# A graph network in which the second middle attention layer goes from gathered edges to a dense sum over all sources

## The chip, the cores and the metric

One core of one Trainium2 chip. The time is device microseconds of one execution of the program; the median of three runs is given. Five engines work side by side and wait for each other through semaphores: PE (TensorE, matmuls), DVE (VectorE), ACT (ScalarE), POOL (GpSimd) and SP (SyncE, here only a DMA queue). The chip has 128 partitions in SBUF and PSUM, and PSUM has 8 banks of 512 fp32 columns.

## The reference

The graph has 3125 nodes with 256 features and 103,125 directed edges (50,000 random pairs in both directions, and a loop at every node). Four graph layers follow each other, each with a residual and a layer norm: a transformer convolution, a relation layer, a two-step graph attention ("L2") and a last layer with attention and a scan. The change is about the second attention of L2 (one head), cut here to what is computed:

```python
feat = h1 @ fc2_w.T                                   # [n, 256]
el = sum(feat * attn_l2, -1); er = sum(feat * attn_r2, -1)
e  = leaky_relu(el[src] + er[dst], 0.2)
ex = exp(e - segment_max(e, dst)[dst])
a  = ex / segment_sum(ex, dst)[dst]
h2 = segment_sum(feat[src] * a, dst) + bias2
x  = layernorm(x + h2 + norm * (concat([inputs, h1]) @ wb1.T + bb1))
```

An edge that occurs twice counts twice in both sums.

## The kernel before, in words

Nodes are sorted by the number of their edges and laid into T = 25 tiles of P = 128 (NP = 3200 places). Every node of a tile is one partition. `build_slots` writes for each tile a list of records to a scratch tensor `slots`: one record holds 16 source numbers for each of the 128 nodes, as two chunks of S = 8. The most connected node of a tile sets how many chunks the tile has; there are 116 chunks in all, in 64 records.

The program then runs stages, each closed by `finish` (clear the semaphores, a barrier of all engines): count edges, order nodes, project and build the slots, and the layers `conv`, `rel`, `gat1`, `gat2`, `last`, `join`. Three of them are made by one function, `edge_layer` (line 907), with other sizes. Per chunk in `gat2`, `gather` on POOL (line 1012) issues 8 indirect DMAs (line 1021), each of which fetches for all 128 nodes one source row of 257 numbers (256 features and el) from DRAM. SP loads the 8 source numbers and the mask of a chunk (lines 995, 998). DVE makes the logits (`logits`, lines 1086 to 1092), ACT the exponentials (line 1252), and DVE multiplies the 8 rows by their weights (line 1100) and adds them up (a reduce that reads with a step of 256 numbers, lines 1110 and 1112), with a running maximum and rescaling (lines 1113 to 1127). Three buffers of rows let POOL run ahead. At the first two chunks of a tile the tile before is finished: division, bias, the part held in `kp["a"]`, residual, norm (lines 1135 to 1158, 755, 756), PE transposes the new x and multiplies it by the next layer's weights (lines 724, 732), ACT copies the result to `stage`, POOL scatters it to DRAM (lines 1030, 1034). Everything is fp32. The order on each engine is the order of the program; there is no planner.

`count_edges` (line 108) already counts by one-hot products: DVE compares bf16 numbers with a row of iotas (line 183), and PE multiplies the two one-hot matrices (line 221).

## Time and profile before

| | |
|---|---|
| median of 3 runs | 7950.94 us (7949.7 to 7951.02) |
| the profiled execution | span 7951.9 us, which is the only time that its page has |
| DVE busy | 5588.3 us, 70% |
| POOL busy | 5351.3 us, 67% |
| PE busy (matmul) | 3326.4 us, 42% |
| ACT busy | 1251.3 us, 16% |

The page gives busy time over the whole span; the stages have different limits, so it is read by stretch. "PEclk" is TensorE's granted clock in tenths of 2.4 GHz: 5 means 1.2 GHz. In a timeline, a row is a start and a duration; consecutive instructions on one engine overlap a little, so what an instruction costs in a chain is the distance from its start to the next start. On SP and in rows with a q behind the engine the duration is the issue alone.

### The profile page before, as it was taken

How to read it: one execution, taken by the hardware profiler on the slowest of the kernel's cores; microseconds unless marked ns; L12 is line 12 of the kernel's file. 1: busy time of each engine (PE TensorE's matmuls, PEld its weight loads, DVE VectorE, ACT ScalarE, POOL GpSimd, SP SyncE). 2: the span in 40 equal slices, each digit the busy share in tenths (PEclk: the TensorE clock that was granted, in tenths of full speed). 3: DMA queues.
4: the chain of work that ended last, by engine and by line, in shares of the span. 5: the costliest groups of instructions: out<-in, count | busy, mean ns of one | idle time of the engine just before them, and what ended most of it. 6: DMA issues, size and time to landing. Idle time of an engine off the chain costs nothing. (4 is left out here: it accounts for less than half of the span.)

```text
span 7951.9 us, 73782 instructions
## 1 busy us (share of the span) xinstructions
PE 3326.4 (42%) x15180; PEld 2659.3 (33%) x15181; DVE 5588.3 (70%) x11215; ACT 1251.3 (16%) x2729; POOL 5351.3 (67%) x4985
## 2 busy tenths in 40 slices
PE   3445454444677767212222200000025555555556
PEld 3233333334666666101111100000024444444434
DVE  7578888884333343688888677777766778777756
ACT  3101111111011111000000000001022332222312
POOL 0667676665777777577777677777757777776521
PEclk7766767667878888555555555555557787777767
DMA  2346656552332332233333233333322333333210
GB/s 84 88 129 169 165 154 166 161 142 76 85 88 84 86 88 76 64 92 97 88 98 93 65 79 98 90 89 98 86 82 84 112 105 104 107 103 96 76 35 13
DMA packets 489232, 773.99 MB, mean 97 GB/s; under 512 B 298796, under 2 KB 319767, under 8 KB 485436
## 3 DMA queue, kind: packets, MB, share of 16 engines
q0 software_dynamic: 265920, 667.09, 30.5%
q10 hardware_dynamic: 20536, 77.34, 2.6%
q1 hardware_dynamic: 202688, 28.69, 2.3%
q14 instruction: 69, 0.57, 0.0%
q8 instruction: 19, 0.31, 0.0%
HBM read 823.08 MB, written 46.52 MB: 109 GB/s over the span
## 5 line engine op out<-in xcount | busy, mean ns | idle before, releaser
L1021 POOL DMA_INDIRECT gat_rows<-scratch_gat,gat_index x1856 | 1858.4, 1001 | 583.4 <-issue 542.4
L1934 POOL DMA_INDIRECT m_rows<-scratch_gat,m_index x928 | 1217.9, 1312 | 508.8 <-issue 272.9
L1021 POOL DMA_INDIRECT conv_rows<-scratch_kv,conv_index x928 | 929.8, 1002 | 424.4 <-issue 252.1
L1467 POOL DMA_INDIRECT rel_rows<-scratch_x,rel_index x928 | 1016.0, 1095 | 295.4 <-issue 279.4
L1317 PE MATMUL conv_ps<-conv_work,k_ident 128*128 128x256 f32 x1856 | 679.2, 545 | 751.1 <-DVE conv_work L1100 679.5
L724 PE MATMUL gat_ps<-k_ident,gat_cur 128*128 128x128 f32 x100 | 34.5, 448 | 2127.7 <-DVEq L1184 1201.7
L1317 PEld LDWEIGHTS conv_ps<-conv_work,k_ident 128*128 128x128 f32 x1856 | 520.5, 288 | 910.2 <-issue 721.1
L724 PEld LDWEIGHTS gat_ps<-k_ident,gat_cur 128*128 128x128 f32 x100 | 14.5, 203 | 2163.3 <-DVEq L1184 1220.1
L1732 PE MATMUL rel_ps<-rel_factor,rel_rows 128*128 128x128 f32 x3712 | 600.3, 338 | 270.6 <-DMA rel_rows<-scratch_x,rel_index 270.3
L1732 PEld LDWEIGHTS rel_ps<-rel_factor,rel_rows 128*128 128x128 f32 x3712 | 582.5, 251 | 282.7 <-DMA rel_rows<-scratch_x,rel_index 175.1
L1112 DVE TENSOR_REDUCE gat_red<-gat_work 128x256 f32<-128x2048 f32 x182 | 652.4, 3584 | 0.0
L1100 DVE TENSOR_TENSOR gat_work<-gat_rows,gat_psprob 128x2048 f32<-128x2048 f32 x232 | 530.8, 2288 | 61.9 <-ACT gat_psprob L1252 50.4
L1990 PE MATMUL m_ps<-m_work,k_ident 128*128 128x256 f32 x1664 | 491.6, 464 | 172.3 <-DVE m_work L2224 172.3
L1990 PEld LDWEIGHTS m_ps<-m_work,k_ident 128*128 128x128 f32 x1664 | 391.1, 240 | 261.2 <-issue 190.9
L1974 PE MATMUL m_ps<-m_hs,k_ident 128*128 128x128 f32 x1600 | 281.9, 358 | 318.8 <-DVEq L2193 318.8
L1974 PEld LDWEIGHTS m_ps<-m_hs,k_ident 128*128 128x128 f32 x1600 | 272.4, 270 | 333.6 <-DVEq L2193 333.6
L1252 ACT ACTIVATE gat_psprob<-gat_logit 128x72 f32<-128x72 f32 (+1 forms) x232 | 48.2, 208 | 2129.7 <-DVE gat_logit L1092 2129.7
L1083 DVE TENSOR_TENSOR conv_dots<-conv_rows,conv_psown 128x2048 f32<-128x2048 f32 x116 | 265.4, 2288 | 84.2 <-DMA conv_rows<-scratch_kv,conv_index 36.6
L2224 DVE TENSOR_TENSOR m_work<-m_rows,m_ps 128x2048 f32<-128x2048 f32 x104 | 238.0, 2289 | 80.2 <-ACT m_ps L2056 80.2
L1100 DVE TENSOR_TENSOR conv_work<-conv_rows,conv_psprob 128x2048 f32<-128x2048 f32 x116 | 265.2, 2286 | 21.4 <-ACT conv_psprob L1252 20.4
L1084 DVE TENSOR_REDUCE conv_logit<-conv_dots 128x64 f32<-128x2048 f32 x116 | 265.2, 2286 | 4.0
L1528 DVE TENSOR_TENSOR rel_ps<-rel_ps,rel_norm 128x128 f32<-128x128 f32 x65 | 19.3, 296 | 321.4 <-PE rel_ps L1720 321.3
(488 smaller groups left out, 7569.5 us busy)
## 6 DMA issues: line engine op xcount, KB each, us to landing
m_bc<-scratch_bc ACTq DMA_DIRECT2D x25, 2048.0 KB, 8.6
gat_rows<-scratch_gat,gat_index POOLq DMA_INDIRECT x1856
conv_rows<-scratch_kv,conv_index POOLq DMA_INDIRECT x928
rel_rows<-scratch_x,rel_index POOLq DMA_INDIRECT x928
m_rows<-scratch_gat,m_index POOLq DMA_INDIRECT x928
scratch_runs<-e_runs_sb ACTq DMA_DIRECT2D x1, 6453.1 KB
scratch_runs<-e_runs_sb SPq DMA_DIRECT2D x1, 6437.5 KB
scratch_kv<-p_row ACTq DMA_DIRECT2D x25, 256.0 KB, 2.5
```

The source lines that it names most:

```text
L1021: pool.indirect_dma_start(out=rows[b][:, s, :], out_offset=None, in_=table, in_offset=bass.IndirectOffsetOnAxis(ap=index[b][:, s:s + 1], a ...
L1083: st.do(v.tensor_tensor(dots[:], rows[b][:, :, 0:F], over_slots(own[:], S), ALU.mult))
L1084: st.do(v.tensor_reduce(lg, dots[:].rearrange(per_head, h=H), X, ALU.add))
L1100: v.tensor_tensor(work[b][:].rearrange(per_head, h=H), rows[b][:, :, values:values + F].rearrange(per_head, h=H), over_dims(prob[:, 0:S, : ...
L1112: st.add(v.tensor_reduce(red[:], slots, X, ALU.add))
L1317: ins = pe.matmul(ps_sum[min(b, 1)], ident, work[b][:, s, :], start=s == 0, stop=s == S - 1)
L1467: pool.indirect_dma_start(out=rows[b][:, g, :], out_offset=None, in_=dr["x1"], in_offset=bass.IndirectOffsetOnAxis(ap=index[b][:, g:g + 1] ...
L1732: ins = pe.matmul(ps_sums[h * 2 + g // 4][:, (g % 4) * P:(g % 4 + 1) * P], rows[b][:, g, h * P:(h + 1) * P], factor[b][:, g * BASES:(g + 1 ...
L1934: pool.indirect_dma_start(out=rows[b][:, s, :], out_offset=None, in_=dr["gat3"], in_offset=bass.IndirectOffsetOnAxis(ap=index[b][:, s:s + ...
L1974: ins = pe.matmul(ps_y[:, k, :], kp["ident"][:], hs[:, k, n, :], start=n == 0, stop=n == NS - 1)
L1990: ins = pe.matmul(ps_sum[bank_of(b)], kp["ident"][:], work[b][:, s, :], start=s == 0, stop=s == S - 1)
L2224: v.tensor_tensor(work[b].rearrange(per_head, h=H), rows[b][:, :, 0:F].rearrange(per_head, h=H), over_dims(prob[:, 0:S, :], D), ALU.mult). ...
```

## The change

`gat2` leaves the list of layers. A new stage `count_pairs` after `build_slots` makes, per tile of 128 destinations, a table over all 25 × 128 sources: `ln(1.001 * edges + 1e-18)`, and very low where there are no edges. It goes to a new DRAM scratch tensor `pairs` (25 × 1.6 MB). A new stage `dense_layer` at the place of `gat2` holds all 3200 source rows in SBUF (`table`), loads one slice of `pairs` per tile, makes the logits of all sources against the 128 destinations, takes the maximum per destination, exponentiates, and sums with 25 fp32 matmuls of 128 sources each; a column of ones in the table gives the denominator. Sources are on the partitions, destinations and source tiles along the free axis, so a logit tile is 128 × 3200 with the source tile h as the innermost index. Both stages are written out over the tiles (`for t in range(T)`) on DVE and ACT.

```diff
-    "gat2": dict(heads=1, width=F + 1, table="gat2", values=0, limit=NP - 1),
...
             def node_numbers(st, t):
-                v.wait_ge(written, 16 + 16 * (1 + scans) * t)
+                v.wait_ge(written, 16 + 16 * t)
                 st.add(v.tensor_copy(node[:, 0:1], kp["info"][:, bass.ds(t, 1), 0]))
-                st.add(v.tensor_copy(node[:, 1:2], kp["info"][:, bass.ds(t, 1), 3]))
...
+D8 = 8
+BANK_DSTS = 20
+def count_pairs(nc, dr, kp):
+    G, HALF = P // D8, P // D8 // 2
+    KEYS = D8 * T
...
+            def load_record(r):
+                rows = dr["slots"][bass.ds(r * 2, 2) if not isinstance(r, int) else slice(0, 2)]
+                for k in range(2):
+                    sp.dma_start(record[:, :, k, :], rows[k].rearrange("(g d) w -> g d w", d=D8)[:, :, 2 * S:3 * S]
+                                 ).then_inc(sems["record_in"], 16)
...
+            def spread_record(r):
+                st = new_steps(v, sems["steps"])
+                v.wait_ge(sems["turned"], r + 1)
+                st.do(v.tensor_copy(src_i[:], ps_record))
+                v.sem_inc(sems["taken"], 1)
+                st.do(v.tensor_scalar(rest_i[:], src_i[:], P - 1, None, ALU.bitwise_and))
+                st.add(v.tensor_copy(rest[:], over_dims(rest_i[:], 2)))
+                st.add(v.scalar_tensor_tensor(key[:], over_dims(src_i[:], 2), base[:], over_dims(rest_i[:], 2), ALU.add,
+                                              ALU.subtract))
+                st.wait()
+                for half in range(2):
+                    groups = slice(half * HALF, (half + 1) * HALF)
+                    v.wait_ge(summed[half], r + 1)
+                    for ones_at, number, numbers, w in ((hot_low, rest, low_no, P), (hot_key, key, key_no, KEYS)):
+                        ins = v.tensor_tensor(
+                            ones_at[:, groups, :].rearrange("p g (j z) -> p g j z", z=2),
+                            number[:, groups, :].unsqueeze(2).to_broadcast([P, HALF, w // 2, 2]),
+                            over_slots(numbers[:], HALF).rearrange("p g (j z) -> p g j z", z=2), ALU.is_equal)
+                    ins.then_inc(hot[half], 1)
+            def let_fall(t):
+                x = logs[t % 2]
+                v.wait_ge(sems["freed"], COUNT_BANKS * (t + 2))
+                v.scalar_tensor_tensor(x[:], x[:], FALL, x[:], ALU.mult, ALU.min).then_inc(sems["fallen"], 1)
+            for t in range(T):
+                lo, hi = record_range(v, t)
+                spread_record(lo)
+                if t:
+                    let_fall(t - 1)
+                with v.If(hi > lo + 1):
+                    with v.Fori(lo + 1, hi) as r:
+                        spread_record(r)
...
+                for b in range(COUNT_BANKS):
+                    pe.wait_ge(sems["freed"], t * COUNT_BANKS + (b + 1))
+                    pe.matmul(bank[b][:, 0:bank_columns(b)], zero[:, 0:P], zero[:, 0:bank_columns(b)], start=True,
+                              stop=False, skip_group_check=True)
+                with pe.Fori(lo, hi) as r:
+                    pe.wait_ge(sems["taken"], r + 1)
+                    turn_record(r + 1)
+                    for half in range(2):
+                        pe.wait_ge(hot[half], r + 1)
+                        for g in range(half * HALF, (half + 1) * HALF):
+                            for b, to, to_end, of, of_end in bank_pieces(g):
+                                ins = pe.matmul(bank[b][:, to * T:to_end * T], hot_low[:, g, :],
+                                                hot_key[:, g, of * T:of_end * T], start=False, stop=False,
+                                                skip_group_check=True)
...
+                for b in range(COUNT_BANKS):
+                    act.activation(out[:, at:at + n], bank[b][:, 0:n], ACT.Ln, bias=tiny[:], scale=ABOVE_ONE
+                                   ).then_inc(sems["freed"], 1)
...
+def dense_layer(nc, io, dr, kp):
...
+            sp.dma_start(table[:], dr["gat2"].rearrange("(h p) w -> p h w", p=P)).then_inc(sems["table_in"], 16)
...
+            def mask(t):         
...
+                by_tile = z[:].rearrange(by_node, h=T)
+                for h in range(T):
+                    st.add(v.tensor_scalar(by_tile[:, :, h], er_rows[:, t * P:(t + 1) * P], el[:, h:h + 1],
+                                           el_low[:, h:h + 1], ALU.add, ALU.max))
+                st.wait()
+                v.wait_ge(pairs_in[t % 2], 16 * (t // 2 + 1))
+                v.tensor_tensor(z[:], z[:], pairs[t % 2][:], ALU.add).then_inc(sems["masked"], 1)
+                v.wait_ge(sems["masked"], t + 1)
+                v.tensor_reduce(column[:], z[:].rearrange(by_node, h=T), X, ALU.max).then_inc(sems["column_top"], 1)
+            def find_top(t):
+                v.wait_ge(sems["column_turned"], t + 1)
+                st.do(v.tensor_reduce(top[:], ps_column, X, ALU.max))
+                v.tensor_scalar(diag[0][:], kp["ident"][:], top[:], None, ALU.mult).then_inc(sems["top"], 1)
+            def lower(t):
+                v.wait_ge(sems["top_spread"], t + 1)
+                v.tensor_tensor(z, z, over_dims(ps_top, T), ALU.subtract).then_inc(sems["lowered"], 1)
...
+                act.activation(weight[t % 2], logit[t % 2][:].rearrange("p (d h) -> p h d", h=T), ACT.Exp
+                               ).then_inc(sems["weights"], 1)
...
+                for h in range(first, end):
+                    ins = pe.matmul(ps_out[t % 2], weight[t % 2][:, h, :], table[:, h, :], start=h == 0, stop=h == T - 1)
...
-        for name in ("conv", "rel", "gat1", "gat2", "last", "join"):
+        count_pairs(nc, dr, kp)
+        for name in ("conv", "rel", "gat1", "dense", "last", "join"):
```

In `count_pairs` SP loads one record ahead, PE turns it (`turn_record`, 16 partitions to 128), DVE spreads it; each of the two halves has its own buffer and its own semaphore. `bank_pieces` splits the 16 groups of 200 keys where a bank of 20 destinations ends, into 19 matmuls. ACT also issues the store of each finished slice.

In `dense_layer` the order of iteration t is written out by hand. DVE: `mask(t + 1)`, `new_rows(t - 2)` (node numbers, normalise), `take_sum(t - 1)` (reciprocal, scale, add the base), `find_top(t + 1)`, `stats(t - 1)`, `lower(t + 1)`. ACT: `weigh(t)` (the exponential), `turn_rows(t - 2)`, `stage_rows(t - 2)`, `root_of(t - 1)` (a square root). PE: sources 0 to 7 of tile t, the transpose of the column maxima of t + 1 (`turn_column`), sources 8 to 12, `spread_top(t + 1)` (the maxima onto all partitions), the transposes of the new x of t - 2, sources 13 to 18, `project(t - 2)`, sources 19 to 24. POOL first makes the bases (`kp["a"] * inv_deg + x + bias2`, three operations of 256 columns per tile), then the scatters. SP loads the next slice of `pairs` as soon as the one before the last is used. `COUNTS` gets one step fewer per tile for `conv` and `gat1`.

## Rows read from the trace of the kernel before

**Rows 1.** The page: span, busy time of each engine, granted clock of TensorE in slices.

```profile
span 7951.9 us, 73782 instructions
PE 3326.4 (42%) x15180; PEld 2659.3 (33%) x15181; DVE 5588.3 (70%) x11215; ACT 1251.3 (16%) x2729; POOL 5351.3 (67%) x4985
...
PEclk7766767667878888555555555555557787777767
```

**Rows 2.** Timeline (start us, duration us): where the layer begins and ends.

```profile
4539.33 0.34 SPq L982 DMA_DIRECT2D gat_v_L_gnn_bias<-in_L_gnn_bias  x1
...
5844.59 0.96 POOL L1034 DMA_INDIRECT scratch_scan_x<-gat_cur,gat_node  x1 [0.30 <-issue]
5854.68 0.40 SPq L1896 DMA_DIRECT2D m_win<-in_in_proj  x1
```

**Rows 3.** Groups by line in that layer: xcount, busy us, mean ns, idle before.

```profile
L1021 POOL DMA_INDIRECT gat_rows<-scratch_gat,gat_index x928 | 929.6, 1002 | 292.1 <-issue 271.2 <-DMA gat_index<-scratch_slots 11.7 <-DVE gat_work L1100 9.3
L1112 DVE TENSOR_REDUCE gat_red<-gat_work 128x256 f32<-128x2048 f32 x91 | 325.9, 3581 | 0.0
```

**Rows 4.** Busy time by stretch: second attention, last layer, edge counting; granted clock follows POOL.

```profile
4539.00:5855.00 1316.00, 70.41 (x150) 36.57 (x150) 1014.29 (x2101) 115.62 (x291) 981.68 (x982) 0.50 0.33 87
5855.00:7600.00 1745.00, 962.87 (x4206) 810.46 (x4206) 1328.63 (x2832) 491.76 (x1204) 1221.08 (x934) 0.76 0.33 97
60.00:139.00 79.00, 47.52 (x1218) 45.09 (x1218) 74.28 (x75) 15.98 (x23) 0.00 (x0) 0.83 0.31 132
```

**Rows 5.** Timeline of DVE in the edge counting.

```profile
52.37 0.98 DVE L183 TENSOR_TENSOR e_hotdh<-e_partdh,e_io 125x1600 bf16<-125x1600 bf16 x1
53.27 1.22 DVE L183 TENSOR_TENSOR e_hotdl<-e_partdl,e_io 125x2048 bf16<-125x2048 bf16 x1
54.41 0.98 DVE L183 TENSOR_TENSOR e_hotsh<-e_partsh,e_io 125x1600 bf16<-125x1600 bf16 x1
```

**Rows 6.** DMA issues by line: count, size, us to landing.

```profile
rel_record<-scratch_slots SPq DMA_DIRECT2D x65, 24.0 KB
m_bc<-scratch_bc ACTq DMA_DIRECT2D x25, 2048.0 KB, 8.6
```

**Rows 7.** Timeline of DVE: between two passes of a loop, and between two tiles.

```profile
4502.02 0.17 DVE L1127 TENSOR_TENSOR gat_den<-gat_den,gat_part 128x8 f32<-128x8 f32 x1
4503.14 0.23 DVE L1086 TENSOR_TENSOR gat_logit<-gat_rows,gat_own 128x64 f32<-128x64 f32 x1 [0.96 <-DVE gat_den L1127]
...
6232.47 0.17 DVE L2290 COPY k_top<-m_top 128x4 f32 x1
6234.82 0.06 DVE L2249 MEMSET m_den<- 128x4 f32 x1 [2.17 <-issue]
```

**Rows 8.** Groups by line on DVE: 3200 columns, and 2048 columns read in order.

```profile
L1556 DVE SCALAR_TENSOR_TENSOR rel_junk<-rel_keyall,rel_mine,rel_behind 128x3200 bf16<-128x3200 f32 x25 | 88.7, 3546 | 0.1
L1084 DVE TENSOR_REDUCE conv_logit<-conv_dots 128x64 f32<-128x2048 f32 x116 | 265.2, 2286 | 4.0
```

**Rows 9.** Timeline of DVE: back-to-back operations with two per-partition scalars each.

```profile
6208.58 0.60 DVE L2117 TENSOR_SCALAR m_cv<-m_seq,m_cw,m_cb 128x128 f32<-128x128 f32 x2
...
7644.98 1.70 DVE L2522 TENSOR_SCALAR j_hl<-j_u,j_moments,j_inv 128x256 f32<-128x256 f32 x5
```

**Rows 10.** Groups by line on ACT: a table load, a strided write, a write in order.

```profile
L766 ACT ACT_TABLE_LOAD x50 | 64.2, 1283 | 0.9
L203 ACT ACTIVATE e_runs_sb<-e_nrm 125x413 f32<-125x413 f32 x16 | 16.1, 1005 | 0.0
L373 ACT ACTIVATE n_sign<-n_degall,n_above 128x2816 bf16<-128x2816 f32 x1 | 2.6, 2625 | 0.0
```

**Rows 11.** Timeline of PE: fp32 products of 256 columns, two products to a row.

```profile
7663.03 2.07 PE L732 MATMUL j_ps<-j_wl,j_hlt 128*128 128x256 f32 x4 [1.33 <-ACT j_hat L2443]
...
7672.12 1.03 PE L732 MATMUL j_ps<-j_wl,j_hlt 128*128 128x256 f32 x4
7672.99 1.03 PE L732 MATMUL j_ps<-j_wg,j_hat 128*128 128x256 f32 x4
```

More of the change, by code:

```diff
@@ L1286, in finish_tile @@
                     next_rows(t, ps[2])
-                elif layer == "gat2" and place == 0:
-                    root_of(act, sems, small, t + 1)
-                elif layer == "gat2":
-                    turn_new_x(t)
             def first_pair(t):
@@ L2623, in network @@
                 edge_layer(nc, io, dr, kp, name)
-COUNTS = {"conv": (11, 2, 3, 19, 0), "gat1": (13, 1, 4, 9, 8),
-          "gat2": (13, 1, 8, 13, 8)}
+COUNTS = {"conv": (11, 2, 3, 18, 0), "gat1": (13, 1, 4, 8, 8)}
 DIRECT = ["x", "src", "dst", "edge_type_32", "edge_weight1", "node_vec",
```

357 lines of the change are left out of this document (323 added, 34 removed).

## The prediction

> **What bounds the kernel now.** I read the page first: DVE is busy 70% of 7951.9 us and POOL 67%, and the granted clock of TensorE has a long run of fives in its middle [rows 1]. An average over six stages says little, so I cut the span at the stage borders with the timeline. The layer that goes, `gat2`, issues its first DMA at 4539.33; the next layer issues its first at 5854.68, 10.1 us after the start of the last scatter [rows 2]. So the stage is 1315.35 us long, drain and barrier included. Inside it the groups by line show what sets the pace: POOL issues 928 gathers of 1.002 us, 929.6 us, and stands 292.1 us between them, 271.2 of it "issue", which is its own sequencer [rows 3]. That is 1.30 us per gather and 1221.7 in all. DVE is busy 1014 of 1316 us there, PE 70, at a granted clock of 0.50 [rows 4]. The bound is POOL's issue; DVE is next. The change takes both away here, so the question is only what the two new stages cost.
>
> **The sum's frame.** It is made against the profiled execution, whose page gives only its span, 7951.9 us. The median of the runs, 7950.94, is 1.0 us less, so nothing has to be added around the span.
>
> **Removed:** 1315.4 us, from first issue to first issue [rows 2].
>
> **Added, `count_pairs`.** Records: the relation layer loads 65, one ahead of its need [rows 6], so 64, or 2.56 per tile; 25 are first ones of a tile, 39 run in the inner loop. DVE per record: the compare has the form of line 183 (bf16, one input repeated), where 1600 columns take 0.90 us start to start and 2048 take 1.14 [rows 5], 0.536 ns per further column. A half record is 8 x 128 = 1024 columns (0.59) and 8 x 200 = 1600 (0.90), two halves 2.98 us. Before them stand four tiny operations, at 0.17 to 0.2 each with their waits (line 1127 takes 0.17 [rows 7]): 0.8. So 3.8 us. Going round a loop costs DVE 0.95 us (4502.19 to 4503.14), and from tile to tile, with register loads, 2.2 us (6232.64 to 6234.82) [rows 7]. `let_fall` is one operation on 3200 fp32 columns, 3.5 us by line 1556 [rows 8]. A tile is 3.8 + 2.2 + 3.5 + 0.95 + 1.56 x (3.8 + 0.95) = 17.9 us. Beside it on PE: the edge counting has 1218 bf16 matmuls of 64 columns in 47.5 us, 39 ns each at a clock of 0.83 [rows 4], thus at most 2.0 us for the 3200 columns of a record and some 3.3 at half clock, below DVE's 4.75. The one new wait in the chain is `let_fall` on ACT: after DVE's last half PE needs 1.6 more and seven closing matmuls, then ACT seven logarithms of 500 columns. ACT takes 2.625 us for 2816 columns [rows 10], 0.93 ns each, some 0.28 of it fixed and overlapped, so about 0.6 each, 4.1 together; all seven are done 6.2 us after DVE's last compare, while DVE itself needs 6.0 to come there (2.2 + 3.8). 0.2 us is left over. Behind that waiting instruction only DVE's next record is queued. The store of 1.6 MB per tile fits: 2 MB land in 8.6 us [rows 6], with 18 to spare. 25 x 18.1 = 452, 5 to begin, 7 for the last store and 10 for its own barrier (the 10.1 us of [rows 2]): **474 us**, taking PE's clock at half and all loop costs. Bounds: 380 if the register loads hide (3.8 + 3.5 + 1.56 x 3.8 = 13.2 per tile, and 50 around), 580 if PE, ACT and DVE alternate (22 per tile, 30 around).
>
> **Added, `dense_layer`.** DVE per tile, in its order. `mask`: 25 operations of 128 fp32 columns with two per-partition scalars. Two such with a write in order take 0.60 us, five of 256 columns 1.70 (0.32 apart) [rows 9], so the lower bound is 0.26 apart, 6.5 us. But here each number is written 100 bytes from the last. No row has that on DVE. The nearest are the reduce of line 1112, which reads 2048 columns 1024 bytes apart in 3.581 us [rows 3], where line 1084 reads as many in order in 2.286 [rows 8] (1.67 against 1.04 ns per number), and on ACT line 203, which writes 413 numbers 128 bytes apart in 1.005 us [rows 10], 1.98 per number without the fixed 0.19. I take the reduce's 1.67: 128 x 1.67 = 0.21 plus 0.2 fixed is 0.42, and 25 of them 10.4 us; with 1.98, 11.3. Then add the pairs (3.5) and reduce (3.5), both in order [rows 8]; `new_rows` 0.9, `take_sum` 1.1, `find_top` 0.7, `stats` 0.8 (each of the operations that `gat2` does today); `lower` 3.5; waits 0.6. Sum 25.0 us. The low end, with free strides, is 21.
>
> The Trainium skill speaks on both sides of this step. Its page "SBUF — State Buffer", section "Door 1: The DMA port swizzle", says that SBUF works in lines of 16 bytes and that every access on a new line pays, which is against the change's layout, written and read 100 bytes apart; the reduce of line 1112 bears it out for reads, at 1.67 ns, and no run here shows DVE writes. Its page "VectorE: DVE Perf Modes", section "What auto-detection actually checks", grants a single-source fp32 operation in SBUF two elements per cycle by shape alone, whatever the step; by that rule `mask` would be the 6.5 us of the low bound, and the tile 21.
>
> PE per tile: 25 products of 256 (257) fp32 columns. At full clock two take 0.87 us (7672.12 to 7672.99), at half 1.9 (7663.03 and on) [rows 11]: 10.9 us or 23.3, with transposes, top and projection 13 or 28. Which clock: 13 of 25 us busy is 52%; the last layer has 55% and 0.76, the edge counting 60% and 0.83, `gat2` 5% and 0.50 [rows 4]. PE will pause twice per tile, so I take the half clock for the first group of 8 sources (7.5 us) and full for the rest. ACT: the exponential reads 3200 numbers 100 bytes apart; in order it would be 2.9 us (2816 in 2.625), by the stride of [rows 10] up to 6.1; I take 5.5. One table load (1.283 [rows 10]) stands on each side of the square root.
>
> The hand order makes a ring: project(t - 2) 0.9, stage 0.6, load and root 1.5, load 1.3, exponential 5.5, then 19 of 25 products, and among them the small PE work (1.1) until the next project; its waits are some 1.5. Full clock: 6.9 + 5.5 + 8.2 = 20.6; first 8 at half: 24.6; all at half, the small PE work too: 8.4 + 5.5 + 17.7 = 31.6. With DVE's 25.0 as the other ring they meet at `spread_top(t + 1)`, behind 13 products: weights of t are ready 9.5 us after `lower(t)`, 8 products at half end at 17, the column maxima come at 17.5, 5 products more end at 20 to 22, DVE is there at 20.3. So 25 to 27, and I take **26 us** per tile. 24 full iterations are 624. Before them: table of 3.3 MB and first slice, by 2 MB in 8.6 us some 20 us with short rows; first mask and the rest of its chain 26: 46. After them: exponential, 25 products, take, norm, projection, scatter, drain and the barrier: 43. Together **713 us**. POOL's 75 small operations lie beside the first tiles; take_sum needs one base per 26 us. Bounds of the stage: 24 x 21 + 80 = 584, and 24 x 32 + 101 = 869. SP's loads of `pairs` (8 us) lie under the 26.
>
> **COUNTS:** 50 copies of one number leave DVE in `conv` and `gat1`, at 0.07 apart: 3 us.
>
> **Sum:** 7951.9 - 1315.4 + 474 + 713 - 3 = 7820.5, so **7820 us**, 1.6% faster. The gain is small because 1315 us of issue are replaced by 1187 of dense work.
>
> **Rivals.** *Strides are free and PE stays fast.* The tile is 21 us, DVE's own sum: 7951.9 - 1315.4 + 474 + 584 - 3 = 7690. For it: the 2 columns per cycle of small scaled operations (five of 256 in 1.70). Against it: the reduce of line 1112. *PE stays at half clock: the slower side.* The clock of a stretch falls when PE pauses, and PE waits here for ACT's exponential and for the column maxima in every tile, and a paused PE has shown 0.5 to 0.8 in this trace. Then the ring project, root, exponential, 19 products turns once in 31.6 us and sets the tile, not DVE: dense 24 x 32 + 101 = 869, the whole 7975, slower by 24 us. It decides from 31.0 us per tile on: 24 x 31.0 + 101 + 474 - 3 = 1316. For it: `gat2`'s stretch has 0.50. Against it: at half clock PE would be busy 28 of 32 us, and the edge counting, busy 60%, already has 0.83 [rows 4]. *The counting compares one number per cycle.* 5248 columns a record at 1.04 ns instead of 0.54 add 2.6 us, 168 us in all: 7990. Against it: line 183 has the very form. *The two new stages stay as they are but less hides in counting* (22 us per tile): 7925.
>
> **How the numbers follow.** Forecast 0.50, cheap strides 0.17, half clock 0.14, slower counting alone (to 7925) 0.14, one number per cycle 0.05. The forecast's own range is 7760 to 7880. The range takes in the cheap strides and reaches almost to the half clock: 7670 to 7960. A measurement of this kernel tells some 16 us (0.2%) from nothing. Faster than 7935: 0.50 + 0.17 + most of 0.14 = 0.79; within: 0.04; slower: 0.17.
>
> **What would show it.** In the changed profile: no gather between the first attention and the last layer; `count_pairs` some 474 us with DVE over 80% busy and PE near 0.5 to 0.6; one `mask` operation every 0.42 us (0.26 would be the cheap rival); the exponential 5.5 us; the distance of two `lower` 26 us, with DVE's idle time before it small; PE's clock 0.7 to 0.8 in the dense stretch. I am wrong in kind if the gap before `lower` is several us (PE sets the tile), or if DVE in `count_pairs` waits for the record's DMA.

## The result and the profile after

The changed kernel takes 7648.6 us (median; 7642.8 to 7652.0), the kernel before, on the same chip, 7950.3. The ratio is 0.961 with an interval of 0.957 to 0.965: 302 us less, where I had forecast 131 less (7820) and a range down to 7670. The sign was right, the size was not. Of all the executions reported below one was slow, at a granted clock of 0.55 (7874.8 us, a run of the last version), and it is left out.

The page of the changed kernel: its span, busy times and two of its slice rows (answering [rows 1]):

```profile
span 7648.5 us, 76632 instructions
PE 3913.1 (51%) x18186; PEld 3106.7 (41%) x18187; DVE 5414.7 (71%) x10644; ACT 1490.0 (19%) x2823; POOL 4505.8 (59%) x4131
...
PEclk7776677677668888888555555578867878777767
```

The run of fives in TensorE's clock is shorter, and POOL's share has gone from 67% to 59%. For the stages I cut at the first DMA that each issues, by the timeline (start, duration, queue, line), as in [rows 2]:

```profile
423.11 1.38 SPq L1384 DMA_DIRECT2D c_record<-scratch_slots  x2
...
823.48 0.37 SPq L978 DMA_DIRECT2D conv_v_L_gnn_gamma<-in_L_gnn_gamma  x1
...
4935.34 0.39 SPq L1556 DMA_DIRECT2D d_table<-scratch_gat  x1
...
5550.90 0.38 SPq L2314 DMA_DIRECT2D m_win<-in_in_proj  x1
```

The counting runs from 423.11 to 823.48, **400.4 us** (forecast 474), the dense stage from 4935.34 to 5550.90, **615.6 us** (forecast 713). Together 1016.0 for the 1315.4 removed. All other stages together are 4.0 us shorter (7951.9 - 1315.4 + 1016.0 - 7648.5), where I had 3. So the whole error of 171 us lies in the two new stages: 74 in the counting, 97 in the dense one. The windows of the counting, of the dense stage and of its stretch from the first `lower` to the last, against [rows 4] (columns as named in the first line):

```profile
core 0: us, PE busy (x) PEld busy (x) DVE busy (x) ACT busy (x) POOL busy (x), PEclk, DMA share, GB/s
423.00:823.00 400.00, 269.22 (x1631) 171.14 (x1631) 325.13 (x543) 97.11 (x176) 0.56 (x3) 0.64 0.27 104
4935.00:5551.00 616.00, 390.66 (x1525) 319.56 (x1525) 523.23 (x1037) 251.83 (x204) 126.33 (x125) 0.78 0.23 84
4977.00:5507.00 530.00, 349.50 (x1376) 287.90 (x1377) 482.33 (x946) 233.17 (x174) 93.29 (x90) 0.80 0.22 79
```

Now one turn of the dense loop, from one `lower` to the next, in the timeline; DVE, ACT and PE are mixed, and "xN" merges neighbours:

```profile
5204.23 3.49 DVE L1636 TENSOR_TENSOR d_logit<-d_logit,d_ps 128x3200 f32<-128x3200 f32 x1 [0.93 <-PE d_ps L1734]
...
5207.63 6.66 DVE L1620 TENSOR_SCALAR d_logit<-d_errows,d_el,d_ellow 128x128 f32<-128x128 f32 x25
...
5208.41 1.28 ACT L766 ACT_TABLE_LOAD   x1
...
5211.23 6.24 ACT L1690 ACTIVATE k_b<-d_logit 128x3200 f32<-128x3200 f32 x1
...
5217.52 5.16 PE L1742 MATMUL d_ps<-d_table,k_b 128*128 128x257 f32 x16 [7.00 <-ACT k_b L1690]
5217.86 3.49 DVE L1626 TENSOR_REDUCE d_column<-d_logit 128x128 f32<-128x3200 f32 x1
...
5222.52 0.27 PE L1730 MATMUL d_ps<-k_ident,d_column 128*128 128x128 f32 x1
...
5225.22 3.49 DVE L1636 TENSOR_TENSOR d_logit<-d_logit,d_ps 128x3200 f32<-128x3200 f32 x1 [0.54 <-PE d_ps L1734]
```

DVE goes from `lower` to the 25 mask operations, the pairs, the reduce and the small ones almost without a pause, in 20.99 us. The 24 distances between two `lower` are 22.1 us on average (4976.43 to 5507.01); in the steady part they go round in threes, 21.0, 22.4 and 21.5. ACT shows the order that costs: stage, table load (5208.41), root, table load, and only then, at 5211.23, the exponential of logits that stood lowered since 5207.7. PE's first eight products follow it, 16 instructions in 5.2, 5.7 or 6.6 us at part clock (3.7 would be full clock, as a run below shows), and so the column's transpose (5222.52) comes more than a microsecond after the reduce that it waits for. From the fifth tile on `lower` waits 0.5 to 0.9 us for PE in every turn, and in two turns of three the maximum before it waits 0.2 to 1.2 us too. The first two distances are longer, 28.8 and 27.6 us; a run below shows why. The two groups:

```profile
L1636 DVE TENSOR_TENSOR d_logit<-d_logit,d_ps 128x3200 f32<-128x3200 f32 x25 | 87.2, 3488 | 24.3 <-PE d_ps L1734 24.3
L1690 ACT ACTIVATE k_b<-d_logit 128x3200 f32<-128x3200 f32 x25 | 154.2, 6169 | 56.5 <-DVE d_logit L1636 56.2
```

One turn of the counting, two records (the same columns):

```profile
783.75 0.68 ACT L1498 ACTIVATE c_logs<-c_ps,c_tiny 128x500 f32<-128x500 f32 x1 [9.27 <-PE c_ps L1478]
...
787.62 3.49 DVE L1433 SCALAR_TENSOR_TENSOR c_logs<-c_logs 128x3200 f32<-128x3200 f32 x1 [1.78 <-ACT c_logs L1498]
...
791.03 0.17 DVE L1413 CAST c_srci<-c_ps 128x16 int32<-128x16 f32 x1
...
794.94 0.17 DVE L1413 CAST c_srci<-c_ps 128x16 int32<-128x16 f32 x1
```

A record is 3.90 us from start to start (791.03 to 794.94), with no pause where the loop turns or the next tile's registers are loaded. `let_fall` (787.62) waits 1.78 us for ACT's seven logarithms (the first at 783.75, the other six in 3.26 us, so some 0.54 apart), which ACT starts only when PE has closed the tile.

### The profile page after: what moved, and what is told of

Read it like the earlier page. It is cut to its first block and busy times, and to the rows that moved or that the text cites. A ratio compares the mean times of both kernels' runs of the same rounds, so it can differ in the third digit from the quotient of the medians.

```text
span 7648.5 us, 76632 instructions
## 1 busy us (share of the span) xinstructions
PE 3913.1 (51%) x18186; PEld 3106.7 (41%) x18187; DVE 5414.7 (71%) x10644; ACT 1490.0 (19%) x2823; POOL 4505.8 (59%) x4131
## 5 line engine op out<-in xcount | busy, mean ns | idle before, releaser
L1017 POOL DMA_INDIRECT gat_rows<-scratch_gat,gat_index x928 | 929.0, 1001 | 291.3 <-issue 273.9
L724 PE MATMUL gat_ps<-k_ident,gat_cur 128*128 128x128 f32 x50 | 17.2, 448 | 926.8 <-DVE gat_cur L1143 926.8
L1742 PE MATMUL d_ps<-d_table,k_b 128*128 128x257 f32 x1250 | 345.9, 436 | 171.2 <-ACT k_b L1690 171.2
L1742 PEld LDWEIGHTS d_ps<-d_table,k_b 128*128 128x128 f32 x1250 | 271.8, 223 | 229.8 <-ACT k_b L1690 181.2
L1104 DVE TENSOR_REDUCE gat_red<-gat_work 128x256 f32<-128x2048 f32 x91 | 326.6, 3590 | 0.0
L1571 POOL DMA_INDIRECT scratch_gat<-d_stage,d_node x25 | 36.8, 1473 | 456.1 <-ACT k_er L1703 456.1
L1092 DVE TENSOR_TENSOR gat_work<-gat_rows,gat_psprob 128x2048 f32<-128x2048 f32 x116 | 265.4, 2288 | 33.5 <-ACT gat_psprob L1231 27.6
L1092 DVE TENSOR_TENSOR conv_work<-conv_rows,conv_psprob 128x2048 f32<-128x2048 f32 x116 | 265.2, 2286 | 21.4 <-ACT conv_psprob L1231 20.4
```

Of the source, the lines that this page charges most:

```text
L1017: pool.indirect_dma_start(out=rows[b][:, s, :], out_offset=None, in_=table, in_offset=bass.IndirectOffsetOnAxis(ap=index[b][:, s:s + 1], a ...
L1092: v.tensor_tensor(work[b][:].rearrange(per_head, h=H), rows[b][:, :, values:values + F].rearrange(per_head, h=H), over_dims(prob[:, 0:S, : ...
L1104: st.add(v.tensor_reduce(red[:], slots, X, ALU.add))
L1742: ins = pe.matmul(ps_out[t % 2], weight[t % 2][:, h, :], table[:, h, :], start=h == 0, stop=h == T - 1)
```

## The experiments

They ran in five groups. In three of them the kernel before takes 7950 us, in two 9121 to 9123, and the time lies in the gather stages that no run touches (conv to gat1's start 3164 us against 2819 in the changed kernel, last layer to the end 2515 against 2098), while the two new stages are the same within 3 us: 402.8 and 613.7 there. The texts put on record before the runs call this two chips, and that is not shown: the record numbers the chips 0, 6, 3, 1 and 6, and number 6 stands once beside 9121 and once beside 7949. What differs is open; below it is called the slower place. So each experiment is read by the length of its stage, first DMA to first DMA, against 400.4 to 402.8 for the counting and 613.5 to 615.6 for the dense stage.

**The mask written in order.**
```diff
-by_tile = z[:].rearrange("p (d h) -> p d h", h=T)
-v.tensor_scalar(by_tile[:, :, h], er_rows[...], el[...], el_low[...], ALU.add, ALU.max)
+v.tensor_scalar(z[:, h * P:(h + 1) * P], er_rows[...], el[...], el_low[...], ALU.add, ALU.max)
```


> The 25 mask operations of a tile write their 128 numbers in order instead of 100 bytes apart (the logits then stand in another place than the pairs; the output is not the layer's). My prediction took a stride at 1.67 ns per number and 0.42 us per operation; the changed kernel shows 0.266 from start to start. Theory A: the stride of a write costs DVE nothing and the operation is 0.2 fixed plus 128 numbers at two per cycle: 0.266 stays, the dense stage stays at 615.6 us within 3, the whole at 7648 within 10. Theory B: part of the 0.266 is still the stride, and in order it is 0.20 or less: 25 x 0.066 x 25 = 41 us less, some 7607, if DVE sets the tile.

Measured: dense stage 613.5, the whole 7649. The mask operations, of the changed kernel and then of this one (duration min/median/max in ns):

```profile
L1620 DVE TENSOR_SCALAR d_logit<-d_errows,d_el,d_ellow x625: 375/408/960, 4954.7 to 5494.2; 128x128 f32<-128x128 f32 x157
```

```profile
L1619 DVE TENSOR_SCALAR d_logit<-d_errows,d_el,d_ellow x625: 329/344/893, 4958.1 to 5498.3; 128x128 f32<-128x128 f32 x157
```

A single one is shorter in order, 344 against 408 ns, but 25 of them take 6.50 us against 6.66: they start 0.256 and 0.260 apart. At 100 bytes the stride changes the duration and not the pace. Theory A for the time, though its reason did not hold (below).

**The exponential read in order.**
```diff
-logit[t % 2][:].rearrange("p (d h) -> p h d", h=T), ACT.Exp
+logit[t % 2][:].rearrange("p (h d) -> p h d", h=T), ACT.Exp
```


> The exponential reads its 3200 numbers in order instead of 100 bytes apart (the weights then belong to other sources; the output is not the layer's). It takes 6.17 us in the changed kernel. Theory A: ACT pays for a strided read of fp32, in order it takes 2.9 to 3.3 us (0.93 ns per number), and since DVE sets the tile with 20.5 us of its own, the tile goes from 21.6 on average only to 20.8 to 21.2: the stage 10 to 20 us shorter. Theory B: ACT, exponential and PE form the ring that sets the tile: it goes down by the whole 3 us, 24 x 3 = 72 us less. Theory C: the stride is free on ACT as on DVE and 6.17 us is what 3200 exponentials cost: nothing changes.

```profile
L1690 ACT ACTIVATE k_b<-d_logit 128x3200 f32<-128x3200 f32 x25 | 71.8, 2871 | 59.5 <-DVE d_logit L1636 59.3
```

The exponential goes from 6.17 to 2.87 us, DVE's wait before `lower` from 24.3 to 9.2, the stage to 588.0: 26 to 28 us less. Of 3.3 us per tile one third reaches the time, the part by which PE had been late. Theory A, somewhat above its range.

**Without the shift** (reduce, `find_top`, `lower` and their two products on PE left out; the denominator gets a floor).
```diff
-v.tensor_reduce(column[:], ...); find_top(t + 1); lower(t + 1)
-act.wait_ge(sems["lowered"], t + 1)
+act.wait_ge(sems["masked"], t + 1)
```


> Left out: the column maxima, the top and its subtraction (the reduce, find_top, lower, and their two small products on PE), so DVE has 7.4 us less per tile, 13.1 us instead of 20.5; the softmax keeps its value without the shift. Theory A, the ring of my prediction: behind DVE stands project, stage, root with its two table loads, exponential (6.2), 19 products (8.8 at full clock), 20.2 us in all: the tile goes from 21.6 to 20 to 21 and the stage is only 20 to 45 us shorter. Theory B: only DVE sets the tile: 13.1 plus a wait, 24 x 7.4 = 178 us shorter. If PE falls to half clock while it waits, the ring is 25 to 31 us and the stage becomes longer by up to 200.

Stage 560.6, 53 to 55 less. The distance of two pairs additions is 19.4 us on average, but that takes in five short ones at the start (12.8 to 17.9); from the seventh on it is 20.4 to 20.8:

```profile
5223.52 3.49 DVE L1624 TENSOR_TENSOR d_logit<-d_logit,d_pairs 128x3200 f32<-128x3200 f32 x1
...
5243.97 3.49 DVE L1624 TENSOR_TENSOR d_logit<-d_logit,d_pairs 128x3200 f32<-128x3200 f32 x1
```

DVE's waits (total us, times, longest):

```profile
DVE d_small L755 <- ACT d_small L766: 97.2, 23, 17.6
DVE d_logit L1620 <- ACT k_b L1682: 84.2, 19, 4.5
```

DVE lost 7.4 us of work per tile and got 181 us of waiting for ACT's root and exponential. The ring of the forecast is there, at 20.5 us at a granted clock of 0.83 (I had 20.2 at full clock): it is as long as DVE's own sum of 20.3, not behind it. Theory A in kind; the gain is 8 to 10 us above its range, which had not reckoned with the short distances at the start.

**The bases beside the reduce.**
```diff
-for t in range(T):
-    a = kp["a"][:, t, :]
+def base(t):
+    pool.wait_ge(sems["masked"], t + 1)
+    a = kp["a"][:, t, :]
...
-for t in range(T): scatter(t)
+base(0)
+for t in range(T + 2): base(t + 1); scatter(t - 2)
```


> The 75 small POOL operations that make the base of each tile are not issued all at the start of the dense stage but three per tile, each behind the tile's pairs addition, so beside DVE's reduce. In the changed kernel the mask takes 12.1, 12.7 and 11.9 us in the first three tiles, while POOL works, and 6.6 in all others. Theory A: POOL's operations hold DVE up (mask doubles, reduce and lower don't): mask is 6.6 in the first tiles too, the distance of the first two pairs of lowers falls from 28.8 and 27.6 to 21 to 23, the head by 5: 15 to 20 us shorter, about 7631. Theory B: the first tiles are slow for the clock of PE or for the loads of the table: no change, and the mask keeps 12 us.

The changed kernel's second tile, POOL and DVE side by side:

```profile
4979.83 12.69 DVE L1620 TENSOR_SCALAR d_logit<-d_errows,d_el,d_ellow 128x128 f32<-128x128 f32 x25
...
4992.56 3.86 DVE L1624 TENSOR_TENSOR d_logit<-d_logit,d_pairs 128x3200 f32<-128x3200 f32 x1
4993.15 3.85 POOL L1584 TENSOR_TENSOR k_a<-k_a,d_v_L_gnn_bias 128x256 f32<-128x256 f32 x1
...
4996.45 3.49 DVE L1626 TENSOR_REDUCE d_column<-d_logit 128x128 f32<-128x3200 f32 x1
...
4997.98 0.72 POOL L1583 TENSOR_TENSOR k_a<-k_a,k_x 128x256 f32<-128x256 f32 x1
```

The mask takes 12.69 us where it takes 6.6 later, POOL's addition is held for the whole of the pairs addition (3.85 us instead of 0.72), and beside the reduce neither is slower. With POOL moved there:

```profile
4966.28 3.49 DVE L1642 TENSOR_TENSOR d_logit<-d_logit,d_ps 128x3200 f32<-128x3200 f32 x1 [0.89 <-PE d_ps L1740]
...
4969.68 6.56 DVE L1626 TENSOR_SCALAR d_logit<-d_errows,d_el,d_ellow 128x128 f32<-128x128 f32 x25
...
4986.11 3.49 DVE L1642 TENSOR_TENSOR d_logit<-d_logit,d_ps 128x3200 f32<-128x3200 f32 x1 [1.78 <-PE d_ps L1740]
```

The whole 7620.7 (7618.9 to 7623.9), the stage 590.5, 25 less. Theory A. The gain is above my range because the first two distances fell to 19.8 us, where I had expected 21 to 23: that is 17 us; the head is 6 us shorter and the tail 2. The rule fits what the Trainium skill says ("SBUF — State Buffer", section "Who interferes with whom"): the second port pair of DVE is POOL's only one, an operation with one tensor input and scalars takes it in its fast mode, an operation with two inputs in SBUF contends with POOL's reads, a reduce and an operation with at most one SBUF input (`lower` has the other in PSUM) do not. The trace agrees on all four: 12.69 us for 6.6, 3.85 for 0.72, and 3.49 for both the reduce and `lower` (4976.43) with POOL at work beside them.

**A drained queue in the counting.**
```diff
 ins.then_inc(hot[half], 1)
+st.do(v.memset(last[:], 0.0))      # one column, and DVE waits for it
```


> In the counting stage one tiny operation (one column) is put behind the last compare of each record, and DVE waits for its end before it goes on: the queue is empty when the loop turns or the registers of the next tile are loaded. My prediction charged 0.95 us per loop turn and 2.2 per tile for these; the changed kernel shows 0 (records 3.90 us from start to start, 400 us in all). Theory A: the loop and the register loads cost what I took, but they run beside compares that are still queued; drained they come back: 39 turns x (0.95 + 0.2) and 25 x (2.4 less the 1.9 that DVE waits for ACT anyway): 45 to 60 us more, 7695 to 7710 in all. Theory B: in this stage the loops are cheap whatever is queued: only the tiny operation and its wait, 64 x 0.2 less what ACT's wait hides, 8 to 13 us more.

```profile
DVE c_srci L1414 <- DVE c_last L1430: 42.0, 35, 1.6
DVE c_logs L1435 <- ACT c_logs L1500: 7.1, 7, 5.7
DVE c_srci L1414 <- remote: 6.0, 3, 2.0
```

The stage is 413.7, 11 to 13 us more, the number of theory B. But the rows show A's mechanism: 48 us of pauses have appeared at 38 places (42.0 behind the added L1430, 6.0 "remote"), 0.58 us at a turn of the loop and 1.6 to 2.0 from tile to tile, and 41 have gone before `let_fall`, which DVE now reaches when ACT is done. I had counted 64 places; behind `let_fall`, 3.5 us long and not drained, the loop turns unseen, which leaves 14 turns and 24 tiles. So the expectation was wrong in its bookkeeping and right about what hides the loop.

**Without `let_fall`.**
```diff
-v.scalar_tensor_tensor(x[:], x[:], FALL, x[:], ALU.mult, ALU.min)
```
(The store then waits for the logarithms.)


> let_fall is left out of the counting (absent pairs then stand at the logarithm of 1e-18 instead of minus 1e29). DVE loses its 3.4 us of work per tile and the 1.9 us in which it waits for ACT's logarithms. Theory A: the operation covers a chain, products, seven logarithms of 0.54 apart, zeroing, transpose of the next record, which ends 2.6 us before let_fall does; so DVE gains 2.5 us per tile and then waits for the next transposed record: 60 to 65 us less, some 7585. Theory B: DVE alone sets the stage: 25 x 5.3 = 133 us less, 7515.

```profile
DVE c_srci L1413 <- PE c_ps L1452: 54.3, 26, 4.4
```

The stage is 333.3, 67 to 70 us less. DVE's wait has moved to the next record's transpose. Theory A, a little above its range.

**`let_fall` in two.**
```diff
+for banks, lo, hi in ((4, 0, 2000), (COUNT_BANKS, 2000, NP)):
+    v.wait_ge(sems["freed"], COUNT_BANKS * (t + 1) + banks)
+    v.scalar_tensor_tensor(x[:, lo:hi], x[:, lo:hi], FALL, x[:, lo:hi], ALU.mult, ALU.min)
```


> let_fall is made in two operations: columns 0 to 2000 as soon as ACT has made the logarithms of four banks, the rest after the seventh. Theory A: DVE's 48 us of idle time before let_fall is the wait for the last of seven logarithms, 0.54 apart; the first part begins three of them, 1.6 us, earlier, the second finds them ready: 35 to 40 us less, about 7610. Theory B: DVE only waits later for the same chain (the next record's transpose stands behind the zeroing, behind the last logarithm): less than 10 us.

```profile
L1435 DVE SCALAR_TENSOR_TENSOR c_logs<-c_logs 128x2000 f32<-128x2000 f32 x25 | 56.0, 2240 | 10.3 <-ACT c_logs L1500 10.0
...
L1435 DVE SCALAR_TENSOR_TENSOR c_logs<-c_logs 128x1200 f32<-128x1200 f32 x25 | 35.0, 1401 | 0.0
```

The idle time before it is 10.3 us instead of 48.2, the stage 363.3: 37 to 40 less. Theory A.

**Rows staged a tile later.**
```diff
-weigh(t); turn_rows(t - 2); stage_rows(t - 2); root_of(t - 1)
+weigh(t); stage_rows(t - 3); turn_rows(t - 2); root_of(t - 1)
```


> ACT's order in the dense stage is changed: the rows of tile t - 3 are staged right behind the exponential of t, so that the root of t - 1 and both table loads no longer wait for PE's projection. The exponential then starts some 3.3 us earlier (right behind lower). Theory A: the 24 us that DVE is idle before lower come from PE being late with the eight products ahead of the column transpose; with the weights 3 us earlier most of it goes, as with the exponential read in order: 15 to 25 us less, about 7628. Theory B: PE's clock falls again because its pause is as long as before, and the wait stays: within 5 us of 7648. In both the scatter of rows comes a tile later, which costs 5 us at the end at most.

```profile
5817.28 3.48 DVE L1636 TENSOR_TENSOR d_logit<-d_logit,d_ps 128x3200 f32<-128x3200 f32 x1
...
5820.80 6.20 ACT L1690 ACTIVATE k_b<-d_logit 128x3200 f32<-128x3200 f32 x1
...
5837.55 3.48 DVE L1636 TENSOR_TENSOR d_logit<-d_logit,d_ps 128x3200 f32<-128x3200 f32 x1
```

The exponential (5820.80) now starts as `lower` ends, PE has its eight products done before the column comes, and `lower` follows `lower` in 20.27 us without a wait: DVE's own sum. Stage 581.2, 33 less; the granted clock from 5550 to 6050 is 0.89, where the changed kernel has 0.82 (below). Theory A, above its range; the tail became 5 to 7 us shorter, not longer.

**The changed kernel again**, as the measure in the slower place.

> The changed kernel once more, beside the others of this call: the stages that an experiment leaves alone can differ from chip to chip (the gathers of the layers left alone, 7950 and 9121 us for the kernel before), so each is compared with this run. Both theories: counting 400 us, dense stage 615 us, as before.

8612.4 us, 0.943 of 9123.0 (0.941 to 0.946): there the change gives 511 us. It removes a gather stage, and the other gather stages are 12 to 20% longer there; that the removed one was too is inferred, as the kernel before has no trace there. The changed kernel's window in its dense stage there, to compare the next run with:

```profile
5550.00:6050.00 500.00, 334.04 (x1329) 275.45 (x1329) 454.57 (x906) 227.23 (x173) 71.28 (x68) 0.82 0.23 83
```

**PE kept busy in its pause.**
```diff
+for _ in range(12): pe.matmul(bank[6][:, 0:F], all_ones[:], w_gat[:, 0, 0:F], start=True, stop=True)
 sum_rows(t, 0, 8)
```


> In each tile of the dense stage 12 products on constant data are put ahead of the first of the 25, into a bank that is free by then: 5.5 us of work in the 7 us in which PE waits for the exponential. Nothing else changes. Theory A: PE's first products run at half clock in two tiles of three because of that pause (16 instructions in 5.2 to 5.7 us instead of 3.7), and this makes the column maxima's transpose late; with the filler the granted clock of the stretch rises from 0.81 to over 0.95, DVE's idle time before lower (24 us) and before top (11) goes to below 10 together: 20 to 30 us less. Theory B: the clock doesn't matter, as the wait comes from the late exponential alone: PE is 8 products behind whatever the clock, within 5 us.

```profile
5550.00:6050.00 500.00, 441.52 (x1990) 366.77 (x1989) 462.15 (x929) 243.89 (x183) 62.80 (x60) 0.98 0.23 81
```

Clock 0.98 for 0.82, stage 590.5, 23 less. Theory A: work that computes nothing made the stage shorter, as the eight products ahead of the transpose then took 3.75 us, full clock. The fall of the clock had cost about 1 us per tile, not the 11 of my slower rival.

**`lower` writes source by source, the exponential in order.**
```diff
-v.tensor_tensor(z, z, over_dims(ps_top, T), ALU.subtract)
+v.tensor_tensor(weight[t % 2].rearrange("p h d -> p d h"), z, over_dims(ps_top, T), ALU.subtract)
+act.activation(weight[t % 2], weight[t % 2], ACT.Exp)
```


> lower reads its 3200 logits in order and writes them 512 bytes apart, source by source, into the buffer of the weights; the exponential then reads and writes in order, in place. Theory A: DVE's strided write is free here too (3.49 us stays), the exponential takes 2.9 instead of 6.2 us: the dense stage 25 to 28 us shorter, as with the exponential read in order. Theory B: a strided write costs an operation with two tensor inputs the 1.6 times that the strided reduce costs, so lower takes 5.6 us: the tile's DVE work is 22.5 us, the stage 20 to 25 us longer.

```profile
L1638 DVE TENSOR_TENSOR k_b<-d_logit,d_ps 128x3200 f32<-128x3200 f32 x25 | 142.8, 5713 | 26.4 <-PE d_ps L1735 26.4
```

`lower` takes 5.71 us for 3.49, the stage 655.1, 41 longer. Theory B in kind, and worse. I had taken the first experiment for "strides are free on DVE", which is more than it showed.

**Four edits together**, that one among them.

> Four edits together: the bases in time, let_fall in two, the rows staged later, lower turned. By the single runs: counting 363 us (37 less); dense: the first tiles without POOL beside them 18 less, the tile at DVE's own sum of 20.3 us instead of 22.1 on average over the rest, 34 less with the tail, and 3 to 6 for the shorter exponential in the first and last tiles, where DVE doesn't cover it: 555 to 562 us. Sum about 93 us less than the changed kernel, 7555 where that is 7648. If DVE isn't all that is left and the edits hide each other, 60 less.

8599.6, 13 less than the changed kernel beside it, which is within the spread of both (8582 to 8623 and 8589 to 8635). The stages are clear: counting at 363.6 as expected, the dense stage at 645.4. The turned `lower` undid the rest, and its stride is not all of it. A tile takes 23.9 us instead of 20.3; 2.2 of that is `lower` itself, and 1.3 is a new wait of `lower` for PE in every tile:

```profile
5724.92 0.47 PE L1740 MATMUL d_ps<-k_ident,d_column 128*128 128x128 f32 x1 [5.22 <-DVE d_column L1634]
...
5725.19 4.05 PE L1752 MATMUL d_ps<-d_table,k_b 128*128 128x257 f32 x10
```

With its weights ready early PE stands still for 5.2 us until the column comes, and the five products between the column and the maxima then take 4.05 us, where in the changed kernel they take 2.34. An exponential that is ready too early has moved PE's pause to a worse place.

**Distance or kind?** Three runs: `lower` with a stride of 100 bytes, in place (`z` as `"p (d h) -> p h d"`); the mask 512 bytes apart (`"p (a b) -> p b a"`, 125 numbers); the turned `lower` with a pitch of 129 numbers.

> lower walks its 3200 logits source by source, so it reads and writes them 100 bytes apart, in place; the result is the same. In order it took 3.49 us; writing 512 bytes apart it took 5.71. Theory A: what costs is the distance: at 100 bytes it is free for this kind of operation too, 3.49 us stays, the dense stage stays at 615 us. Theory B: any stride costs an operation with two tensor inputs, and only the one-input operation of the mask is spared: 5.7 us or more, the stage 45 to 55 us longer.

```profile
L1636 DVE TENSOR_TENSOR d_logit<-d_logit,d_ps 128x3200 f32<-128x3200 f32 x25 | 156.1, 6244 | 7.6 <-PE d_ps L1734 7.6
```

6.24 us, stage 649.4, 34 to 36 longer: theory B in kind, below its range for the stage. The run changes one thing more: the input from PSUM is now read as 128 numbers in order, 25 times over, where it was each number 25 times. How much of the 2.75 us belongs to that, and how much to reading or to writing with the stride, is not shown.

> Each mask operation writes 125 of its 128 numbers 512 bytes apart instead of 100 (the last three columns of each block are left out and the logits stand in other places; the output is not the layer's). Theory A, distance: at 512 bytes each number costs what it costs in lower, 1.78 ns, so the operation takes 0.4 us instead of 0.266, 25 of them 10 us (what I had predicted for 100 bytes), the tile 3.5 us longer and the stage 70 to 85 us longer. Theory B, kind of operation: the one-input operation is spared at any stride: 0.266 stays, the stage within 5 us of 615.

```profile
L1622 DVE TENSOR_SCALAR d_logit<-d_errows,d_el,d_ellow x625: 457/470/495, 4959.6 to 5492.5; 128x125 f32<-128x125 f32 x157
```

Duration 0.47, 25 in 7.95 us, so 0.31 apart; stage 616.0, as DVE's 1.3 us more per tile went into the wait for PE. Between the theories, near B. So at 512 bytes a short operation does pay in pace, 0.05 us more than in order.

> As the kernel whose lower writes source by source 512 bytes apart and whose exponential is in order, but with a pitch of 516 bytes for the weights. Theory A: it is 512 bytes (a power of two) that costs, 516 is as free as 100: lower takes 3.49 us, the exponential 2.87, the stage 25 us shorter than 615. Theory B: it is any distance over some size: lower stays at 5.7 us, the stage at 655 us.

`lower` 5.97 us, stage 665.9: theory B, the power of two is innocent. (For room this run also keeps the logits in one buffer and the weights in buffers of their own.)

**A long operation of the mask's kind**, in order and then strided.
```diff
+st.do(v.tensor_scalar(flat, flat, 1.0, None, ALU.mult))
+v.tensor_scalar(weight[t % 2].rearrange("p h d -> p d h"), z, 1.0, None, ALU.mult)
```


> lower is in order and in place again. Behind it stand two added operations of the mask's kind (one input, a scalar, multiplied by 1.0), each on all 3200 logits: the first in order in place, the second writes source by source, 512 bytes apart, into the weights, where the exponential works in order. Theory A: an operation with one input has its stride free at any length: both take 1.7 to 1.9 us (two numbers per cycle). Theory B: a strided write costs here too, and the mask hides it only because its operations are short (128 numbers), so that a fixed part of one lies beside the end of the one before (start to start 0.266 us at a duration of 0.41): the first takes 1.8, the second 5 to 5.9 us.

```profile
L1641 DVE TENSOR_SCALAR k_b<-d_logit 128x3200 f32<-128x3200 f32 x25 | 93.4, 3736 | 0.9
...
L1640 DVE TENSOR_SCALAR d_logit<-d_logit 128x3200 f32<-128x3200 f32 x25 | 46.1, 1842 | 0.9
```

1.84 us in order, 3.74 strided (L1641); the stage, with both operations added, is 751.6. Theory A falls: a stride of 512 bytes costs the one-input operation too, 1.17 ns per number for 0.58, not the 1.78 of B. B's mechanism, that short operations hide the stride, is not shown by it. At 512 bytes 125 numbers at 0.59 ns more each would be 0.07 us, and the mask at that distance starts 0.05 us later each time, so most of the price is seen in the short operation as well. What hides it at 100 bytes can be the length or the distance: a long operation with one input at 100 bytes was not run.

**The changed kernel and three edits, side by side** (bases in time, `let_fall` in two, rows staged later).

> The changed kernel again, as the measure for the version beside it on the same chip. Both theories: the same time as in its own run on that chip.

> Three edits together on the changed kernel: the bases made beside the reduce, let_fall in two, the rows staged a tile later (lower and the exponential as they are). By the single runs: counting 37 us less, dense stage 34 us less by the order of ACT and 18 by the first three tiles without POOL beside them, which add up as long as DVE's 20.3 us sets the tile: 85 to 92 us less than the changed kernel. If the head and the first tiles are bound by something else once POOL is out of the way, 70.

The changed kernel 7644.9 us, **the three edits 7554.2**: 91 less, 0.950 of the kernel before (0.949 to 0.952). Counting 362.5, dense stage 560.0. Theory A. Its dense window:

```profile
4900.00:5450.00 550.00, 377.21 (x1507) 299.11 (x1505) 498.05 (x1026) 248.67 (x202) 171.62 (x125) 0.89 0.26 91
```

DVE is busy 498 of 550 us, 91%; what is left is its own sum.

## Why the forecast was wrong, step by step

The mechanism was right: DVE sets both new stages, and PE meets it at `spread_top`. Two terms of DVE's sum were mis-sized: the mask, put at 10.4 us per tile and measured at 6.6, and the turns of the loops and the register loads, put at 116 us and measured at nothing.

- **Removed, 1315.4, and the copies in other stages:** right; the other stages gave 4.0 for my 3. (Slips that move nothing: 1221.7 us for 928 gathers are 1.32 each, not 1.30; the rows of the two reduces give 1.75 and 1.12 ns per number, the text's 1.67 and 1.04 leave out 0.16 us each without saying so; the half-clock rival adds up to 7977, not 7975.)
- **The counting's operations:** right. A record is 3.90 us (I had 3.8), `let_fall` 3.49. The trace gives 64 x 3.90 + 25 x 3.41 + 48.2 of waiting = 383, and 17 around.
- **The loop and register costs, 0.95 and 2.2 us: wrong, shown.** They were read where DVE's last operation takes 0.17 us [rows 7]; here compares are queued, and the loop turns beside them. That is 61 + 55 = 116 us of my 474. The drained run brought 48 us back at the 38 places where nothing was queued, at 0.58 and 1.6 us, so both figures were too high for this loop even then.
- **`let_fall`'s wait, 0.2 us per tile: wrong.** It was worked out as covered by those 2.2 us; without them it is 1.93, 48 us in all. The two errors, -116 and +43, make the stage's 74, within 1 us.
- **The mask, 10.4 us per tile: wrong, and 94 of the dense stage's 97 us.** My 0.42 us is the duration of one operation (0.408). I summed durations of operations that overlap: they start 0.260 apart. The stride's price is real in the long operations that were run (3.74 against 1.84 us with one input at 512 bytes, 5.71 to 6.24 against 3.49 with two inputs), but 128 numbers at 100 bytes start as close together as in order. The rows of two and of five in [rows 9] held that pace (0.32 apart at 256 columns), and I used them only for the lower bound. Whether the short length or the short distance spares the mask is open: no run has a long operation with one input at 100 bytes, and none a length between 128 and 3200.
- **The two rules of the Trainium skill.** The rule of the Trainium skill that every access on a new line of 16 bytes pays ("SBUF — State Buffer", section "Door 1: The DMA port swizzle"), which I weighed against the change, agrees with the long operations here (5.71 to 6.24 us for 3.49) and with the mask's duration (0.408 us for 0.344), not with its pace (0.260 for 0.256). The Trainium skill's two elements per cycle whatever the step ("VectorE: DVE Perf Modes", section "What auto-detection actually checks") gave the right mask time, but the long strided operation, at 1.17 ns per number for 0.58 in order, does not bear it out.
- **DVE's other operations, 14.6 us:** 13.7 measured, since these overlap by 0.08 too. DVE's own tile is 20.3 us, not 25.0.
- **PE and the ring: right in place, nearly in size.** PE and DVE meet at `spread_top`, the first eight products run at part clock, the exponential takes 6.17 us (5.5). With DVE at 20.3 the ring adds 1.3 us on average from the fifth tile on; I had allowed 1.0. The filler and the later staging each take it away. The slower rival, 32 us per tile, was nowhere near: the run without the shift has the bare ring at 20.5.
- **POOL's 75 operations, costed at nothing: wrong, 25 us**, an error that made the forecast look better than its terms. I looked whether POOL was in time and not whom it holds up.
- **The ends:** 41.1 and 43.9 for 46 and 43.
- **The range:** the cheap-stride rival had the tile at 21 and the whole at 7690; it was the nearest, with 0.17. Its dense stage (584) and the lower bound of the counting (380) together give 7598, but I took each with the middle of the other, so 7649 fell outside.

## What to carry to other kernels

Cost a row of short operations by the distance of their starts, not by their durations, and a loop turn only where nothing is queued on that engine. Making one engine's step faster can move another engine's pause to where it costs more. Before costing an engine's side work at nothing, look at which operations of the others run beside it. And a stride that cost no time in short operations 100 bytes apart doubled a long one 512 bytes apart: time the length and the distance that will be used.

## What the runs showed of the hardware

- DVE, fp32, in SBUF: one input, 3200 numbers in order 1.84 us, written 512 bytes apart 3.74. Rows of such operations on 128 numbers (125 at 512 bytes) start 0.256 us apart in order, 0.260 at 100 bytes, 0.31 at 512. Two inputs, one of them PSUM: 3.49 in order, 6.24 read and written 100 bytes apart (the input from PSUM in another order too), 5.71 and 5.97 written 512 and 516 bytes apart.
- ACT reading 3200 fp32 numbers 100 bytes apart: 6.17 us, in order 2.87.
- POOL beside DVE: 25 mask operations in 12.69 us for 6.6 while POOL's own kept their 0.72 to 0.93, POOL's addition 3.85 us for 0.72 beside an addition with two SBUF inputs, nothing beside a reduce.
- DVE's loop turns and register loads: no pause with compares queued; with the queue drained 0.58 us per turn and 1.6 from tile to tile.
- PE doing useless products in its pause raised the granted clock from 0.82 to 0.98 and made the stage 23 us shorter.
- The stages made of gathers took 12 to 20% longer in two of the five groups of runs, the two stages without under 1% more or less; what differs is open.
